# Neighbour lists in the nodes' own numbers, made while the adjacency loads, in a four-layer graph attention kernel

## What is computed

```python
h = relu(layernorm(x)); x = x + L0(h, adj)   # additive scores, softmax, batch norm, + h, elu
h = relu(layernorm(x)); x = x + L1(h, adj)   # 4 heads h.h', then a second attention on the heads' result
h = relu(layernorm(x)); x = x + L2(h, adj)   # query.key, leaky relu
h = relu(layernorm(x)); x = x + L3(h, adj)   # additive scores, relu
# inside each: scores = where(adj > 0, e, -9e15); softmax(scores) @ values
```

## Time and profile before

| | us |
|---|---|
| three runs | 1514.72, 1516.84, 1520.01 |
| the profiled execution | 1518.37 |
| its span, first to last instruction | 1516.6 |
| VectorE busy | 1229.1 (81%) |
| TensorE matmuls busy | 952.2 (63%) |
| GpSimd busy | 917.0 (60%) |
| ScalarE busy | 821.5 (54%) |
| mean granted TensorE clock | 0.844 |

### The profile page before, as it was taken

The page is one execution under the profiler, slowest core; times in us unless marked ns, Lnnn a source line. Parts: engine busy times, 40 slices in busy tenths (PEclk is TensorE's granted clock), DMA queues, the critical chain, the costliest instruction groups (busy, mean ns, idle before and its releaser), DMA issues.

```text
span 1516.6 us, 16874 instructions
## 1 busy us (share of the span) xinstructions
PE 952.2 (63%) x4667; PEld 671.9 (44%) x4667; DVE 1229.1 (81%) x1599; ACT 821.5 (54%) x2858; POOL 917.0 (60%) x885
## 2 busy tenths in 40 slices
PE   1027655762599895488899966566616647656572
PEld 0014422321478785477788832222206647632230
DVE  7889677997699999999999348999867998846461
ACT  2025543668176665176686727658974557643220
POOL 2042278721786896189777548886546776437881
PEclk9998887886799998699999988777856767879786
DMA  9961376521222231001110044533115544247666
GB/s 331 240 222 54 91 229 186 167 82 49 91 70 77 78 108 58 30 22 51 48 50 29 15 135 136 145 105 98 55 61 158 178 130 128 71 145 210 181 196 157
DMA packets 101574, 176.89 MB, mean 117 GB/s; under 512 B 47488, under 2 KB 56224, under 8 KB 99424
## 3 DMA queue, kind: packets, MB, share of 16 engines
q0 software_dynamic: 31472, 102.93, 23.2%
q1 hardware_dynamic: 67280, 72.13, 15.2%
q10 hardware_dynamic: 2720, 0.68, 0.2%
HBM read 145.78 MB, written 34.10 MB: 119 GB/s over the span
## 4 chain that ended last, share of the span: by engine, by line
POOL 35%; DVE 21%; issue 19%; PE 12%; ACT 6%; DMA 5%; POOLq 0%; DVEq 0%; SPq 0%; ACTq 0%
POOL big L723 15%; POOL big L696 15%; PE PS L1379 3%; PE PS L1353 2%; ACT big L983 2%; PE PS L1334 2%; DVE big L1664 2%; DVE big L1600 2%; DVE big L1781 2%; DVE big L1785 2%; DMA big<-tab,SI 2%; DMA big<-in_adj 1%; PE PS L1417 1%; POOL big L745 1%; DVE big L1769 1%
## 5 line engine op out<-in xcount | busy, mean ns | idle before, releaser
L723 POOL TENSOR_TENSOR big<-big 128x512 f32<-128x512 f32 x373 | 376.7, 1043 | 160.2 <-DVE big L1742 145.2
L983 ACT ACTIVATE big<-big 128x64 f32<-128x64 f32 x1496 | 371.0, 338 | 153.8 <-DVE big L1742 147.1
L1785 DVE TENSOR_REDUCE big<-big 128x32 f32<-128x2048 f32 (+4 forms) x126 | 297.7, 2362 | 4.3
L1334 PE MATMUL PS<-big,ident 128*128 128x512 f32 x348 | 186.5, 694 | 119.5 <-DVE big L1769 60.4
L1353 PE MATMUL PS<-ident,big 128*128 128x128 f32 x1740 | 232.5, 294 | 38.4 <-POOL big L723 30.7
L1353 PEld LDWEIGHTS PS<-ident,big 128*128 128x128 f32 x1740 | 218.3, 154 | 47.8 <-issue 23.2
L696 POOL DMA_INDIRECT big<-tab,SI x142 | 176.6, 1244 | 78.5 <-issue 39.6
L1777 DVE TENSOR_TENSOR big<-big,PS 128x2048 f32<-128x2048 f32 (+4 forms) x84 | 198.5, 2363 | 17.5 <-PE PS L1365 14.6
L1334 PEld LDWEIGHTS PS<-big,ident 128*128 128x128 f32 x348 | 74.9, 223 | 221.2 <-issue 200.5
L696 POOL DMA_INDIRECT big<-h_rows,SI x142 | 137.4, 968 | 47.6 <-issue 28.4
L1350 PE MATMUL PS<-big,ident 128*128 128x512 f32 x174 | 103.8, 757 | 61.0 <-POOL big L723 56.5
(11 more groups left out here) (182 smaller groups left out, 1598.8 us busy)
## 6 DMA issues: line engine op xcount, KB each, us to landing
big<-in_adj SPq DMA_DIRECT2D x16, 1024.0 KB, 6.1
tab<-big SPq DMA_DIRECT2D x64, 132.0 KB, 1.8
big<-tab SPq DMA_DIRECT2D x32, 264.0 KB, 3.2
h_rows<-big SPq DMA_DIRECT2D x32, 256.0 KB, 2.0
big<-h_rows SPq DMA_DIRECT2D x32, 256.0 KB, 2.9
big<-in_x SPq DMA_DIRECT2D x16, 256.0 KB, 5.1
big<-xs SPq DMA_DIRECT2D x4, 1024.0 KB, 9.3
h_table<-big SPq DMA_DIRECT2D x16, 256.0 KB, 2.1
```

The costliest lines, as they stand in the source:

```text
L723: ins = pool.tensor_tensor(bd(wbuf[:, i % NWB, j, :]), bd(rows[:, k + j, :]), over_d(S[:, h, k + j, :], B), ALU.mult)
L983: ins = act.activation(to, row, ACT.Copy, scale=S[:, h, k + j, b:b + 1])
L1334: mm = pe.matmul(to.rearrange("p (b d) -> p b d", b=B), ident[:, :], rows[:, k, :].rearrange("p (b c) -> p b c", b=B)[:, :, 0:D], start=(k ...
L1785: run(dve.tensor_reduce(scores(u, t)[:, h, k:k + n, :].rearrange("p k b -> p (k b)"), bd(prod[:, 0:n * E]), AX.X, ALU.add))
```

## The change

- **Lists hold node numbers.** `ranked` is the mask times the column number plus one (`codes`, from an iota), which needs no places. So a block's list is made as soon as its mask is there, beside the loading. The masks are in a ring of seven buffers.
- **ScalarE makes the masks** and their degrees (one ACTIVATE with Relu and accum_out for each block, in ScalarE's order between norm steps; `STEPS_WITH`). **GpSimd** takes the diagonal out (two instructions a block). The step that spreads places over columns is gone.
- **x isn't scattered first.** The parts of x are loaded between adjacency blocks (`X_WITH`) into XH, and the first norm runs over nodes in their own order. Each h row is turned back at once (TensorE, then a ScalarE copy beside its x). Ranks are found after block 10's list (`RANKED_AFTER`); TensorE does its part after its row step 8. Then GpSimd scatters info, and x with h as rows of 4 KB. SyncE loads X and H0 (8 MB) at the start of `near()`.
- **Tables stand in the nodes' order.** `tabs[0]` is stored so by the norm. In unit 0 the own rows now are gathered too (one more indirect DMA a tile, 87 for 71). Later tables are scattered into the nodes' order by GpSimd (`put_rows`, 16 indirect DMAs each in units 0, 1, 2 and 3), and a second copy in the order of places (`owns`) is stored by SyncE for `load_self`.
- The turning of H0 in unit 0 is gone.

```diff
-INFO_PARTS = [(0, 8), (8, 14), (14, NT)]
-ROWS_ENDED = {5: [0], 6: [1], 7: [2], 8: [3], 9: [4, 5], 10: [6], 11: [7], 12: [8], 13: [9, 10], 14: [11],
-              15: [12, 13, 14, 15]}
+INFO_PARTS = [(0, 8), (8, 13), (13, NT)]
+RANKED_AFTER = 10
+RANK_STEP = 8
+ROWS_ENDED = {4: [0], 5: [1], 7: [2], 8: [3], 9: [4], 11: [5, 6], 12: [7], 13: [8, 9], 14: [10],
+              15: [11, 12, 13, 14, 15]}
+STEPS_WITH = {2: [0], 4: [1], 6: [2], 8: [3], 10: [4], 12: [5], 14: [6]}
...
+            for c in range(NT):
+                mine = masks[c % len(masks)][:, c * P:(c + 1) * P]
+                pool.wait_ge(mask_made, c + 1)
+                pool.tensor_tensor(own_bits[:, c, :], mine, ident[:, :], ALU.mult).then_inc(own_found, 1)
+                pool.wait_ge(own_found, c + 1)
+                pool.tensor_tensor(mine, mine, own_bits[:, c, :], ALU.subtract).then_inc(own_cleared, 1)
...
+            def send_rows(part):
+                for t in range(*INFO_PARTS[part]):
+                    pool.wait_ge(xh_made, t + 1)
+                    pool.indirect_dma_start(out=xs, out_offset=bass.IndirectOffsetOnAxis(ap=placei[:, t:t + 1], axis=0),
+                                            in_=XH[t], in_offset=None).then_inc(scattered, 16)
             for part in range(len(INFO_PARTS)):
                 send_info(part)
+                send_rows(part)
...
+                        if u == 0:
+                            pool.indirect_dma_start(
+                                out=rowbuf[t % NRB][:, 0:w], out_offset=None, in_=tables[0],
+                                in_offset=bass.IndirectOffsetOnAxis(ap=node[:, t, :], axis=0)
+                            ).then_inc(gathered[t % NRB], 16)
...
+                def put_rows(u, t):
+                    if 0 <= t < NT:
+                        if u == 4:
+                            at = 2 * t % NPS
+                            pool.wait_ge(half_staged, 2 * (NT + t) + 2)
+                            rows, to = nstage[:, at:at + 2, :].rearrange("p i e -> p (i e)"), pair_scattered[t % 2]
+                        else:
+                            pool.wait_ge(*((h_made, t + 1), (h2_out, t + 1), (h_made, NT + t + 1))[u - 1])
+                            rows, to = hring[:, t % NHR, :], hrow_scattered[t % NHR]
+                        pool.indirect_dma_start(out=tables[u], out_offset=bass.IndirectOffsetOnAxis(ap=node[:, t, :], axis=0),
+                                                in_=rows, in_offset=None).then_inc(to, 16)
...
+            def make_mask(c):
+                act.wait_ge(adj_loaded[c % 3], 16 * (c // 3 + 1))
+                if c >= 3:
+                    act.wait_ge(mask_used, max(c - len(masks) + 1, 1))
+                act.activation(masks[c % len(masks)], adjt[:, c % 3, :], ACT.Relu, accum_out=small[:, 0, c:c + 1])\
+                   .then_inc(mask_made, 1)
...
             for c in range(NT):
-                run(dve.tensor_tensor(ranked, mask[:, c, :], places, ALU.mult))
+                dve.wait_ge(own_cleared, c + 1)
+                tell(dve.tensor_tensor(ranked, masks[c % len(masks)], codes, ALU.mult), mask_used, c + 1)
                 for q in range(4):
                     run(dve.max(cand[:, 0, q * 8:(q + 1) * 8], ranked[:, q * (N // 4):(q + 1) * (N // 4)]))
...
+                if c == 1:
+                    make_terms()
+                if c == RANKED_AFTER:
+                    tell_classes()
...
                 for t in ROWS_ENDED.get(c, []):
                     end_row(t)
+                if c == RANKED_AFTER:
+                    find_places()
```

More of the change, by code:

```diff
@@ L108, in gathered_by @@
 def gathered_by(g):
-    return 16 * sum(SLOTS[i % NT] - 1 for i in range(g % NRB, g + 1, NRB))
+    return 16 * sum(SLOTS[i % NT] - (i >= NT) for i in range(g % NRB, g + 1, NRB))
 def heads_job(j):
@@ L161, in program @@
     tables = [tabs[0], h1_rows, h2_table, h3_rows, tabs[3]]
+    owns = [None] + [nc.dram_tensor(f"own{u}", (N, E if u < 4 else B * RW), F32, kind="Internal").ap()
+                     for u in range(1, NU)]
     ctx = ExitStack()
@@ L934, in _ @@
                     act.activation(rT[:, t % 4, :], rT[:, t % 4, :], ACT.Exp, scale=-0.5).then_inc(xvar_rooted, 1)
+            for c in range(NT):
+                make_mask(c)
+                if c == 1:
+                    double_weights()
+                    double_products()
+                for s in STEPS_WITH.get(c, []):
+                    rows_step(s)
+            for s in range(sum(len(v) for v in STEPS_WITH.values()), NT + 6):
+                rows_step(s)
             def near():
@@ L1651, in _, with make_terms @@
-            dve.wait_ge(places_summed, 1)
-            tell(dve.tensor_copy(places[:, 0:2 * E], bank(2, 2)), places_made, 1)
-            dve.wait_ge(places_cast, 1)
+            dve.wait_ge(iota_made, 3)
+            run(dve.tensor_copy(codes, codei))
+            run(dve.tensor_copy(classes, classi))
+            def make_terms():
+                dve.wait_ge(w_copied, 2)
+                for i in range(2):
+                    lo, hi = i * D, (i + 1) * D
+                    for l, wb in enumerate((WB[0], WB[3])):
+                        for to, half in ((D, 1), (D + 1, 0)):
+                            run(dve.tensor_tensor(wtmp[lo:hi, :], wb[lo:hi, 0, i, 0:D],
+                                                  abc[lo:hi, l, half * D:(half + 1) * D], ALU.mult))
+                            ins = dve.tensor_reduce(wb[lo:hi, 0, i, to:to + 1], wtmp[lo:hi, :], AX.X, ALU.add)
+                            if i == 1 and l == 1 and half == 0:
+                                tell(ins, w_terms, 1)
+                            else:
+                                run(ins)
@@ L1655, in end_row, with find_caps @@
+            def find_caps():
+                run(dve.memset(cap, float(BY_RANK[-1])))
+                for t in range(NT - 1):
+                    if BY_RANK[t] > BY_RANK[t + 1]:
+                        run(dve.tensor_scalar(tmp, rank, float(P * (t + 1)), float(BY_RANK[t] - BY_RANK[t + 1]),
+                                              ALU.is_lt, ALU.mult))
+                        run(dve.tensor_tensor(cap, cap, tmp, ALU.add))
             def end_row(t):
                 dve.wait_ge(xvar_rooted, t + 1)
[L1658 removed]
+                if t >= 4:
+                    dve.wait_ge(h0_back, t - 3)
+                tell(dve.scalar_tensor_tensor(h0T[:, t % 4, :], bank(C_BANK[t % 3]), 0.0, rT[:, t % 4, :], ALU.max, ALU.mult),
```

346 lines of the change are left out of this document (175 added, 171 removed).

## The result

The changed kernel took **1539.45 us** (median of 4 runs, 1533.19 to 1544.24), the kernel before 1516.44 on the same chip: ratio 1.0151, 95% interval 1.0116 to 1.0186. That is slower by over 0.3%, as I had called likeliest, but by 23 us where the forecast said 6; it lies near the upper end of the range (1503 to 1541) and outside the forecast's own 1512 to 1532. The profiled execution took 1544.24 us with a span of 1542.4, so it is 4.8 us above the median.

What follows compares the result with a forecast made beforehand. GpSimd had most of the chain (35%), VectorE set the opening, GpSimd's queue led unit 0 up to 262 us. Terms: -23 + 20 + 5 + 3 + 1 = +6 us, so 1523; forecast 1512 to 1532, range 1503 to 1541.

Steps and rivals of the forecast that it cites:

- The opening, -23: Stretch before the first gather: masks, places and x's scatter leave VectorE's path; first gather at 165 for 188.37, gaining 23 us.
- The further 5 us for TensorE at its lower clock: Opening: TensorE idles between most norm steps and so runs slower, adding 5 us before the last row is ended.
- The rivals of the early and the late opening: Early: first gather 139 to 150, time 1497 to 1508, chance 0.2. Late: first gather 178, time 1536, chance 0.15.
- Unit 0, +20 and +5: Unit 0: a loss of 20 us (16 to 25) for added gathers and puts, 5 us for loading X and H0.
- The ten own rows on the leading queue: Unit 0 up to 262 us: ten added gathers on GpSimd's leading queue, 1.25 us each, all on the path.
- The last nine puts lie in waits of 3 to 9 us between centrings and cost nothing: Tail of unit 0: GpSimd's last nine scatters fit into its existing waits, at 0 us.
- The load term: Unit 0: loads of X and H0 beside the gathers cost 5 us (0 to 15), with 297 GB/s at full share.
- loads and gathers share the DMA engines in turns: Rival for unit 0: gathers fall behind by 15 us, not 5, giving 1533; chance 0.15.
- Units 1 to 3, 1 us (0 to 8) and 3 for the starts: 48 added scatters, covered by GpSimd's waits, cost 1 us; the starts of units 2, 3, 4 cost 3 (2 to 6).
- If that cover were gone, each put would cost its 1.25: Units 1 to 3: without GpSimd's idle time, each added scatter would cost 1.25 us, 20 us a unit.
- I am wrong if: Signs of failure: unit 0 grows by less than 12 us, or the first gather is before 155 or after 175.
- Units 1 to 3 as long as now within 3 us each: Sign for the stages after unit 0: each of the three keeps its length to within 3 us.

Runs made afterwards that it cites:

- experiment 8: Kernel before with only the 16 own rows of unit 0 gathered by GpSimd, no scatter: 1530.45 us, ratio 1.0093.
- experiment 10: Kernel before with unit 0's own-row gathers, waits for h_made and scatters, but without the loads of X and H0: 1543.09 us, ratio 1.0170.
- experiment 11: Changed kernel with a copy of 8.4 MB issued ahead of the loads of X and H0 as unit 0 begins: 1554.69 us, ratio 1.0260.
- experiments 12: Changed kernel with all 16 masks made by VectorE again, between its lists, in place of ScalarE: 1570.21 us, ratio 1.0356.
- experiment 1: Changed kernel with the puts of unit 2 one round later (m - 8 for m - 7): 1522.45 us, ratio 1.0040.

## Why the prediction was right or wrong

*The opening, -23: right in its mechanism; that the size is right too is in part luck.* Forecast and found: first gather 165 and 163.4; mask 2.0 and 2.1; VectorE's own work 105.2 and 106.4; waits before the places 11.5 and 6.5, at single rows 2 and 5.5, in the tail 7.5 and 8.5, together 21 and 20.5. The single waits were off by up to 5 us, their sum was not. The further 5 us for TensorE at its lower clock were not there: in the tail one row's matmuls took double time, inside the wait of 4.52 us that is counted already.

```profile
140.95 2.04 PE L1402 MATMUL PS<-big,centring 128*128 128x512 f32 x2 [2.21 <-DVE big L1757]
```

So the last row ended at 152.1, 4 us before the forecast. What followed took 11.3 us, not 8.1, which made most of this good: the turned row, the last scatter of x and the load of info lie behind each other. The rivals of the early and the late opening are both out.

*Unit 0, +20 and +5: the sum right by luck, two terms wrong that cancelled.* The ten own rows on the leading queue were right (12.5 forecast with them alone, 13.1 measured). The step **"The last nine puts lie in waits of 3 to 9 us between centrings and cost nothing"** failed: they cost 7.1, of 13.3 for all puts. (With one put up to 262 us and seven up to 318, there are eight left, not nine; and 11 x 1.25 is 13.75, not 13.9. Neither matters.) I compared the length of a put with the idle time around it, not with its place: the centring stands behind it in the queue, and the put cannot start before `h_made`. The rows in the tail of unit 0, after the change:

```profile
366.14 1.09 POOL L802 DMA_INDIRECT h_rows<-big,SI  x1 [3.42 <-ACT big L1062]
367.26 1.05 POOL L764 TENSOR_TENSOR big<-big,stats 128x512 f32<-128x512 f32 x1
371.74 0.99 POOL L802 DMA_INDIRECT h_rows<-big,SI  x1 [3.42 <-ACT big L1062]
372.76 1.05 POOL L764 TENSOR_TENSOR big<-big,stats 128x512 f32<-128x512 f32 x1
```

and the same two rows in the kernel of experiment 8, with own rows but no puts:

```profile
379.83 1.04 POOL L717 TENSOR_TENSOR big<-big,stats 128x512 f32<-128x512 f32 x1 [3.25 <-DVE stats L1708]
384.13 1.04 POOL L717 TENSOR_TENSOR big<-big,stats 128x512 f32<-128x512 f32 x1 [3.25 <-DVE stats L1708]
```

The centring is no longer started by VectorE's mean, as there, but by the put, and a row takes 5.5 us (372.76 - 367.26) for 4.3 (384.13 - 379.83).

The load term, 5 us, was 0, though its mechanism is real. The estimate of 297 GB/s at full share was too low: 392 GB/s stood in this window, 184 to 204 us, at a share of 1.04 (length, PE, PEld, DVE, ACT, POOL, clock, DMA share, GB/s):

```profile
184.00:204.00 20.00, 13.36 (x21) 5.36 (x22) 15.97 (x43) 9.03 (x34) 16.09 (x13) 0.79 1.04 392
204.00:224.00 20.00, 8.15 (x17) 3.35 (x16) 15.51 (x32) 7.67 (x26) 16.47 (x14) 0.76 0.73 232
```

So the loads are through some 45 us after the unit begins, and until then VectorE waits no more than 2.7 us for any gather behind its first; without the loads, in experiment 10, it is up to 3.4. The rival "loads and gathers share the DMA engines in turns" has in experiment 11 shown that gathers give way to loads; its price in this change, 10 us beyond the 5 forecast, is not there.

*Units 1 to 3, 1 us (0 to 8) and 3 for the starts: this is the step that failed.* Unit 1 was right: its puts are covered. GpSimd's waits for VectorE there (total, times, longest) are 24.3 us shorter than the 103.1 of the earlier trace rows, against some 20 us of puts:

```profile
POOL big L780 <- DVE big L1854: 78.8, 15, 24.5
```

Unit 3 cost 1. The term for the starts was near: from VectorE's last instruction of a unit to the first gather of the next it is 1.0, 1.7 and 2.2 us more at units 2, 3 and 4, together 4.9 for 3. Unit 2 cost 25.4 in the profile, and 19.5 and 15.9 in the kernels of experiments 12 and 11, which have it unchanged; it varies with how the holds fall. The forecast asked whether GpSimd had idle time for 16 x 1.25 us, and found it: "it waits 9.0 us once and 1 to 6 a tile after". Right, and the scatters alone cost nothing (experiment 1). What it did not ask is what its own instruction demands: where a change adds a wait, what is queued behind it, and for whom. It had the facts: that a put waits for `h_made`, some 3 us behind the centring, and that VectorE's and GpSimd's instructions hold each other up. It drew from the second only what happens to the gathers. The other direction, a 0.17 us instruction of VectorE held by a train of GpSimd, was in the trace of before, once and for 8.68 us. The sentence "If that cover were gone, each put would cost its 1.25" prices even the lost cover at 20 us for the scatters, and leaves out the holds.

That the time still lies in the stated range is luck: the range reached up to 1541 for two rivals, a late opening (1536) and gathers held up by the loads (1533), and neither took place. Of the signs that the forecast named, both under "I am wrong if" came out well, since both look at the opening and unit 0; "Units 1 to 3 as long as now within 3 us each" is the one that failed and mattered. Some 11 us of waiting before the places were 6.5, and the four waits of 2 to 4 us in the tail were three of 1.6 to 4.5.

Two readings of the trace of before were off, without effect on the sum. The lists began at 79.19 us, not at 103.9; five of the 16 begin ahead of that time. And three rows, not four, made VectorE wait 2.2 us or more (4.66, 2.33 and 2.21).

For the holds the forecast's rule bears too (the Trainium skill, SBUF — State Buffer, "SBUF: two separate sides"): both inputs of the `nshift` instruction lie in SBUF, and the train reads SBUF. It speaks of one whole instruction, and the rows show more: the hold of 4.73 us ran over five instructions of GpSimd. That it is this lock that holds the small instruction is an argument from the page; the runs show only that the train does.

With the measured stages in place of the forecast's terms: -25.0 + 25.6 - 1.7 + 25.4 + 1.0 + 0.4 = +25.7, the difference of the two profiled spans (25.8).

## What to carry to other kernels

A transfer that is added to an in-order queue has three prices: its own time, its wait, and what stands behind it. Ask for what the queue's next instruction used to start on; if the added wait is younger than that, put the transfer a round later, which here, in units 0, 2 and 3, turned +1.5% into -0.2%. And where two engines hold each other up, as VectorE and GpSimd do here, a short instruction on the critical path should not meet a long train of the other: one more wait, which lets the short one go first, gave 15 us here.

## What was not expected of the hardware

A hold can outlast the instruction of GpSimd that it begins with. In unit 2 of the kernel before and of the changed one: where GpSimd's train had begun 0.1 to 0.2 us before the small instruction, this was released after the train's first instruction or so (0.88 to 0.96 us). Where it began 0.1 to 0.4 us after, with the end of an indirect DMA's issue just ahead of it, the small instruction ended only with the whole train (8.68, 7.39, 6.46, 4.48 and 2.62 us). Where it began 0.55 us before, it was 4.73. Not every meeting led to a hold (one with the train 0.87 us old took 0.19 us in experiment 1). The rule that decides was not found; that a shift of a tenth of a microsecond changes it may be why the same unit 2 took 265 to 275 us.

Gathers on GpSimd and loads on SyncE together moved 392 GB/s, where a stretch of the kernel before had shown 226 at a share of 0.76. Beside the copy of experiment 11 it was 392 again, from 204 to 224 us.
